# An attention and expert block on one core: the query scratch laid out anew, and the start in another order

## What is computed

```
mod = (silu(c) @ wmod)            # per sequence: shift, scale, gate, twice
h = layernorm(x) * (1 + ca) + sa
qkv = (h @ Wqkv.T + bqkv).reshape(B, 16, S, 24)      # a plain reshape
attn = softmax(q @ k.T / sqrt(8)); x = x + ga * ((attn @ v) @ Wo.T + bo)
h = layernorm(x) * (1 + cb) + sb
probs = softmax(h @ router_w.T); top 2 of 8 experts
x = x + gb * sum(w_i * (h @ expert_i + p_i))
```

## Time and profile before

| | |
|---|---|
| median of 3 runs | 556.86 us (556.68 to 558.76) |
| profiled execution | 557.98 us, of which the span in the profile is 556.1 us |
| ACT busy | 494.8 us, 89% |
| PE busy | 519.1 us, 93% |
| first exponential of tile 0 starts | 23.83 us |
| one tile in the loop | 15.7 us |
| packets | 85497, of which under 512 B 61508 |

### The profile page before, as it was taken

One profiled execution on the slowest core, in us unless ns is written; L12 is line 12 of the kernel. 1 busy time (PEld: TensorE's weight loads), 2 busy tenths in 40 slices (PEclk: granted clock), 3 DMA queues, 4 the chain that ended last, 5 costly groups with the idle time before them and its releaser, 6 DMA issues. The chain is left out here.

```text
span 556.1 us, 14357 instructions
## 1 busy us (share of the span) xinstructions
PE 519.1 (93%) x4064; PEld 215.3 (39%) x4064; DVE 362.8 (65%) x1271; ACT 494.8 (89%) x571; POOL 219.2 (39%) x429
## 2 busy tenths in 40 slices
PE   7488889999999999999999999999999999999983
PEld 6233333334343434343433333343434343433352
DVE  4435457677867666677767667677676666664466
ACT  1279989999999999999999999999999999998962
POOL 1223233344443334444443343444433344443335
PEclk9999999999999999999999999999999999999997
DMA  4573333333333333333333333333333332333010
GB/s 100 128 199 90 89 96 78 77 97 88 89 90 89 96 98 84 76 78 93 88 90 90 98 93 83 72 88 91 88 89 95 98 86 65 91 96 84 17 32 14
DMA packets 85497, 48.44 MB, mean 87 GB/s; under 512 B 61508, under 2 KB 76240, under 8 KB 85456
## 3 DMA queue, kind: packets, MB, share of 16 engines
q1 hardware_dynamic: 70162, 43.07, 30.0%
q10 hardware_dynamic: 15294, 4.82, 3.8%
HBM read 32.91 MB, written 14.94 MB: 86 GB/s over the span
## 5 line engine op out<-in xcount | busy, mean ns | idle before, releaser
L547 ACT ACTIVATE probs<-ps_scores 128x1024 f32<-128x1024 f32 x512 | 485.8, 1028 | 42.9 <-DMA q_scr<-qk_parts 19.6
L735 PE MATMUL ps_attn<-probs,values 128*32 128x512 f32 x2048 | 248.1, 599 | 0.4 <-issue 0.4
L717 PE MATMUL ps_scores<-query_stack,key_stack 32*128 32x512 f32 x1024 | 130.7, 500 | 17.5 <-ACT probs L547 11.4
L717 PEld LDWEIGHTS ps_scores<-query_stack,key_stack 32*128 32x128 f32 x1024 | 49.4, 183 | 167.9 <-ACT probs L547 164.1
L422 POOL TENSOR_SCALAR var_eps<-moments 128x1 f32<-128x1 f32 x64 | 12.3, 192 | 222.7 <-DVE moments L1078 149.5
L735 PEld LDWEIGHTS ps_attn<-probs,values 128*32 128x32 f32 x2048 | 54.0, 109 | 110.5 <-issue 110.3
L765 PE MATMUL ps_side<-experts_gated,h2T 128*128 (+1 forms) x228 | 74.7, 409 | 0.0
L1067 DVE RECIPROCAL sums_inv<-sums 128x128 f32<-128x128 f32 x32 | 30.5, 952 | 32.5 <-DMA attnT<-a_scr 32.5
L1074 DVE TENSOR_TENSOR x<-ps_side,x_gated 128x128 f32<-128x128 f32 x31 | 9.0, 292 | 60.8 <-PE ps_side L765 57.2
L1150 DVE TENSOR_TENSOR weighted<-ps_side,coef 128x256 f32<-128x256 f32 x114 | 46.5, 408 | 2.4 <-PE ps_side L765 2.4
L471 POOL TENSOR_TENSOR mix<-weighted 128x512 f32<-128x512 f32 x31 | 39.7, 1280 | 0.0
(11 more groups left out here) (129 smaller groups left out, 498.9 us busy)
## 6 DMA issues: line engine op xcount, KB each, us to landing
key_stack<-k_scr SPq DMA_DIRECT2D x128, 128.0 KB, 2.7
query_stack<-q_scr SPq DMA_DIRECT2D x121, 64.0 KB, 2.2
q_scr<-qk_parts SPq DMA_DIRECT2D x188, 32.0 KB, 2.0
k_scr<-qk_parts SPq DMA_DIRECT2D x64, 64.0 KB, 1.7
a_scr<-attn ACTq DMA_DIRECT2D x126, 18.0 KB
sums<-a_scr SPq DMA_DIRECT2D x32, 64.0 KB, 2.1
attnT<-a_scr SPq DMA_DIRECT2D x32, 64.0 KB, 2.2
out_dram<-out_all ACTq DMA_DIRECT2D x29, 64.0 KB, 1.8
```

Of the source, the lines that this page charges most:

```text
L547: nc.scalar.activation(probs[:, k % RING, g, :], ps_scores[:, slot(k, g), :], ACT.Exp, scale=SCALE)\
L717: mm = nc.tensor.matmul(out_, key_stack[p0:p0 + 32, parity, 2 * k:2 * k + 2, :].rearrange("p j r -> p (j r)"), query_stack[p0:p0 + 32, par ...
L735: mm = nc.tensor.matmul(ps_attn[q:q + 32, :], values[:, parity, g, k, :], probs[:, k % RING, g, h * HALF:(h + 1) * HALF], start=(k == 0), ...
```

## The change

**Scratch.** `q_scr` was `[2, G, 3, 64, R]`: for each half of the partitions and each head three slabs, high, low and high again. Six writes filled it, and a read took 16 rows and each of them together with the row 8 further on. It is now `[G, 2, hd, 2, JH, R]`: the high and the low row of a channel lie side by side. Four writes fill it, each from all 128 partitions. A read takes 16 rows in a row, and takes the whole set twice: its first index is now the repeat (2, step 0), then 16 rows. Before, the first index was 16 rows and the second the pair.

**Transfers.** Of the first tile's four writes ACT issues three and SP one (before four and two). The second tile's query reads go from ACT to the end of SP's prologue, ahead of the load of the remaining x.

**Order of the start.** DVE no longer waits for the value projection before it takes the first q and k from PSUM, since that projection writes to another bank. POOL's `squares` of tile 1 waits until `qk_parts` is done. `hT` of tile 2 is made ahead of the moments of tile 3 and the gate columns. The transposition for tile 3 and the norms of tile 2 move from the end of PE's prologue to behind the first scores of tile 0. `keep_warm` has five new calls, and one with a larger count.

```diff
-    q_scr = nc.dram_tensor("q_scr", [2, G, 3, P // 2, R], F32, kind="Internal").ap()
+    q_scr = nc.dram_tensor("q_scr", [G, 2, hd, 2, JH, R], F32, kind="Internal").ap()
...
-        def write_q(eng, n1, copies=range(6)):
+        def write_q(eng, n1, copies=range(4)):
...
-            for h in range(2):
-                rows = qk_parts[h * R:(h + 1) * R, 0].bitcast(F32).rearrange("p a (g r) -> p a g r", g=G)
-                for place, a in enumerate((0, 1, 0)):
-                    if 3 * h + place not in copies:
-                        continue
-                    eng.dma_start(q_scr[h, :, place].rearrange("g p r -> p g r"), rows[:, a]).then_inc(q_written, 16)
+            rows = qk_parts[:, 0].bitcast(F32)
+            for copy in copies:
+                g, a = copy // 2, copy % 2
+                halves = q_scr[g].rearrange("h d a i r -> a (h d) i r")[a]
+                eng.dma_start(halves, rows[:, a, g * R:(g + 1) * R]).then_inc(q_written, 16)
...
-                    parts = q_scr[h, g].rearrange("s (d i) r -> (s d) (i r)", d=hd)
-                    rows = bass.AP(tensor=parts.tensor, offset=parts.offset, ap=[[HALF, 2 * hd], [hd * HALF, 2], [1, HALF]])
+                    parts = q_scr[g, h].rearrange("d a i r -> (d a) (i r)")
+                    rows = bass.AP(tensor=parts.tensor, offset=parts.offset, ap=[[0, 2], [HALF, 2 * hd], [1, HALF]])
...
-                write_q(sp, 1, (4, 5))
+                write_q(sp, 1, (3,))
...
                 write_q(sp, 2)
                 read_k(2, 1)
+                read_q(sp, 2, 1)
...
             rstd(1, moments1, var_eps1, rstd1, "moments1_done", "var1_done", "rstd1_done")
+            reached(pool, ev["qk_parts_done"], 1)
             squares_of_tile(1)
...
-                    if k == 3 and before == 0:
-                        read_q(act, 2, 1)
...
-            write_q(act, 1, (0, 1, 2, 3))
+            write_q(act, 1, (0, 1, 2))
...
-                keep_warm(2)
+                keep_warm(3)
                 pe.wait_ge(w_loaded, 16)
...
+                if before == 0:
+                    reached(pe, ev["qkT_done"], 2)
+                    a_transpose(3)
+                    a_norms(ps_side[:, P + NE:P + NE + 2 * J], 2)
...
             a_transpose(1)
+            keep_warm(2)
             pe.wait_ge(setup_dve, SETUP_WQKV)
             a_project_qk(1, 0)
-            a_project_v(1, 0, 2 * P)
+            a_project_v(ps_scores[:, 2, HALF:HALF + P], 1, 0)
             setup_columns()
+            keep_warm(2)
...
             a_norms(ps_scores[:, 1, 0:2 * J], 1)
+            keep_warm(1)
             a_normT(ps_scores[:, 1, HALF:HALF + P], 1)
+            keep_warm(4)
             a_transpose(2)
             a_project_qk(2, 1)
-            reached(pe, ev["qkT_done"], 2)
-            a_transpose(3)
-            a_norms(ps_side[:, P + NE:P + NE + 2 * J], 2)
+            keep_warm(4)
...
                 a_hT(0, 1, 0)
                 dve.wait_ge(bias_cols_loaded, 16 * 3)
-                reached(dve, ev["v_ps_done"], 1)
                 a_qk(1)
...
                 a_bounded(ps_scores[0:1, 1, HALF:HALF + P], 1, 0)
+                a_hT(1, 2, 1)
                 a_moments(2, 3)
                 setup_columns()
-                a_hT(1, 2, 1)
```

More of the change, by code:

```diff
@@ L285, in write_q @@
             reached(eng, q_loaded, loaded_before)
-            for h in range(2):
-                rows = qk_parts[h * R:(h + 1) * R, 0].bitcast(F32).rearrange("p a (g r) -> p a g r", g=G)
-                for place, a in enumerate((0, 1, 0)):
-                    if 3 * h + place not in copies:
-                        continue
-                    eng.dma_start(q_scr[h, :, place].rearrange("g p r -> p g r"), rows[:, a]).then_inc(q_written, 16)
+            rows = qk_parts[:, 0].bitcast(F32)
[3 more added lines that the diff above has]
+                eng.dma_start(halves, rows[:, a, g * R:(g + 1) * R]).then_inc(q_written, 16)
         def read_q(eng, n1, parity, stacks=range(4)):
-            q_count, scores_before = times(eng, n1, 96), times(eng, plus(eng, n1, -2), 1)
+            q_count, scores_before = times(eng, n1, 64), times(eng, plus(eng, n1, -2), 1)
             reached(eng, scores_ready[KT - 1][G - 1], scores_before)
@@ L656, in a_project_qk, with a_project_v @@
                 mm.then_inc(ev["qk_ps_done"], 1)
-            def a_project_v(u1, ring, col):
+            def a_project_v(ps, u1, ring):
                 for n in range(G):
                     for odd in range(2):
-                        mm = nc.tensor.matmul(ps_side[odd * R:(odd + 1) * R, col + n * R:col + (n + 1) * R],
+                        mm = nc.tensor.matmul(ps[odd * R:(odd + 1) * R, n * R:(n + 1) * R],
                                               hT[:, ring, n * R:(n + 1) * R], wvT[:, odd].rearrange("p k d -> p (k d)"),
@@ L803, in side1 @@
                 if before >= 2 and after >= 1:
-                    a_project_v(at[2], 1 - parity, P)
+                    a_project_v(ps_side[:, P:2 * P], at[2], 1 - parity)
                 if past < 4 <= before:
@@ L821, in side2 @@
                 if before < 2:
-                    a_project_v(at[2], 1 - parity, 2 * P)
+                    a_project_v(ps_side[:, 2 * P:3 * P], at[2], 1 - parity)
                 if past < 3 <= before:
@@ L1003, in a_qk_parts @@
             def a_qk_parts(n, n1):
-                k_count, q_count = times(dve, n, 32), times(dve, n, 96)
+                k_count, q_count = times(dve, n, 32), times(dve, n, 64)
                 reached(dve, ev["qkT_done"], n1)
@@ L1011, in a_qk_parts, with a_values @@
                 v.tensor_tensor(qk_parts[:, :, 1], qkT[:], qk_parts[:, :, 0].bitcast(F32), ALU.subtract).then_inc(ev["qk_parts_done"], 1)
-            def a_values(u1, ring, col):
+            def a_values(ps, u1, ring):
                 reached(dve, ev["v_ps_done"], u1)
                 v.scalar_tensor_tensor(out=values[:, ring, :, :, 0:hd],
-                                       in0=ps_side[:, col:col + P].rearrange("p (g k d) -> p g k d", g=G, d=hd),
+                                       in0=ps.rearrange("p (g k d) -> p g k d", g=G, d=hd),
                                        scalar=VALUE_SCALE, in1=spread(bv[:], 1, G), op0=ALU.mult, op1=ALU.add)\
@@ L1228, in tile @@
                 if before >= 2 and after >= 1:
-                    a_values(at[2], 1 - parity, P)
+                    a_values(ps_side[:, P:2 * P], at[2], 1 - parity)
                 if past < 3 <= before:
@@ L1239, in tile @@
                 if before < 2:
-                    a_values(at[2], 1 - parity, 2 * P)
+                    a_values(ps_side[:, 2 * P:3 * P], at[2], 1 - parity)
                 if past < 3 <= before:
@@ L1325, in prologue @@
                 value_bias()
-                a_values(1, 0, 2 * P)
+                a_values(ps_scores[:, 2, HALF:HALF + P], 1, 0)
                 head_sums()
```

## The result

The changed kernel takes 586.62 us (median of 6 runs, 585.39 to 589.43), the kernel before 556.77 us (6 runs, 556.59 to 559.08): a ratio of 1.053 (95%: 1.050 to 1.056), 5.3% slower. I had forecast 556.9 us, no change. The profiled execution of the changed kernel took 589.43 us, its span is 587.6.

A forecast was written before the change was run, and what follows sets the result against it. A tile takes what ACT's 16 exponentials take, with PE close behind. Terms: + 1.9 (start) + 0.5 (norms) - 2.0 (reads off ACT) - 0.3 (second tile's reads) = + 0.1 us, forecast 556.9 us, 8-in-10 range 551.5 to 562.

The forecast's parts named there:

- the loop: Term for the loop's tiles: four query reads make attention rows 0 to 1.0 us late, nothing on the path.
- the two engines: Query reads with first index 2 run on two DMA engines of 16; four reads take 7.0 us, not 0.9.
- the slack: In a loop tile, DVE's result for PE may come 1.0 us late at no cost.
- the slower rival: Loop tiles pay for attention rows over 1.0 us late: 560 to 575 us, chance 0.20.
- the loop pays: The slower rival's title: beyond 1.0 us late, each 0.3 us per tile costs 8 us; chance 0.20.
- Reads at the start: First tile's query reads on two engines: first scores at 24.9, 1.9 us later than before.
- First parts: Start, first q and k parts: done at 10.95, 0.5 us gained (0 to 1.4), projection delayed about 0.5 us.
- The case of an early upper level: Start: if added matmuls bring the upper clock level before 8 us, 1.2 us gained.
- Inside tile 0: First tile: 0.5 us lost to moved transposition and norms, 2.0 gained at the ninth exponential by taking reads off ACT.
- The 0.5 us for the norms: Tile 0: transposition and norms behind the first scores cost 0.5 us, bounds 0 and 1.0.
- What would show it: Profile signs: query reads land after 4 to 9 us, scores near 25, unchanged 15.7 us tile, about 8200 packets fewer.
- that mark: Sign in the profile: a query read lands 4 to 9 us after issue; under 3 us would refute the forecast.

The follow-up runs named there:

- 12: 8 with ACT's four attention writes each two exponentials later: 577.47 us, ratio 1.037.
- Experiment 11: 8 with ACT's four attention writes each one exponential later: 555.12 us, ratio 0.997.
- 5: Changed kernel with head 0's query reads split into two transfers of 16 rows each, head 1's left on two engines: 561.84 us, ratio 1.009.
- 8: experiment 3 without the five added keep_warm calls, and one count of 3 back to 2: 555.57 us, ratio 0.9965.
- experiment 3: Changed kernel with each query read issued as two of 16 rows (32 KB each), new scratch and four writes kept: 555.28 us, ratio 0.997.
- experiment 1: Changed kernel with the old scratch, its six writes and 16-row-first reads; new start and second query read on SP kept: 556.10 us, ratio 0.9985.
- experiment 10: experiment 1 with the second tile's query reads back on ACT, behind its 8th exponential: 553.38 us, ratio 0.995.

## Why the prediction was wrong, point by point

*The step that failed* is the loop: "I expect 0 to 1.0 us late, nothing on the path." The mechanism, the two engines, was weighed right and the slack nearly right. The lateness was mis-sized, and with it the term of the sum, which I put at 0: the write lands 1.4 us late where 0.8 were free, and lateness of that size costs some 22 us over all tiles (12). The length of the reading was about right (forecast 8.4 us from the first read's issue to the end, measured 243.4 - 235.84 = 7.6). What I had wrong is what it delays. Against the slower rival I wrote that the last attention write is issued "when most of the reading is over". But its shares on the two engines come through only behind all of the query rows, and SP waits until the whole write has landed. By my own figures the reads ended at 243.3, already 1.1 us past the attention read at 242.18. Here a wait for a transfer was a wait for the slowest of its engines.

*The slack.* Where PE waits, in the changed kernel and in 12, side 0 runs 2.6 us after `sums_inv` starts (249.77 - 247.19); before, 3.36. So 0.8 us were free, where I had 1.0. Experiment 11 fits: with rows 0.5 us late PE still came without a wait (2.83 us), at 555.12. So does 5, with 0.47.

*The price.* The rival "the loop pays" had 0.3 us a tile in its sum and 560 to 575 as its bounds. Lateness alone cost 21.9 us (12 against 8), 0.7 to 0.8 us for each of the loop's and outer tiles; it was 1.6 us there, a little more than in the changed kernel. On top the changed kernel has the 3.0 us of the first reads and the 6.1 us of second gaps in the three spells: 31.0 us, and it is 31.3 slower than experiment 3. That a late side ends in a spell at the lower clock was in none of my cases. Why just these three tiles fell, and none in 12, stays open (PE's longest wait for `weighted` is 2.4 us in the changed kernel and 1.2 in 12).

*Reads at the start.* Forecast 1.9 us later, measured 2.0 (25.87 against 23.83), first scores at 25.04 against 24.9. That it came out so close is partly luck. Without the two engines I had the first scores at 20.5, and experiments 1, 3 and 8 have them at 22.15, 22.30 and 22.18. So the new start gains less than I thought, and the two engines cost some 3 us, not 4.4. The rule of the Trainium skill, "DMA: Bandwidth & Descriptors", section "Why a DMA increments its semaphore by 16 and not by 1", is that a transfer runs on the largest number of engines up to 16 that divides the slowest dimension of both of its sides. For the new reads that is two, and the trace agrees: 14.0% of 16 engines, 2.2, at 41 GB/s.

*First parts.* Forecast done at 10.95, measured 10.61: the two `keep_warm` matmuls moved the projection by 0.09 us (8.10 against 8.01), not 0.5, and DVE's subtraction took 0.43 us in place of 0.72. The case of an early upper level with 1.2 us gained exists: experiment 10's profile shows it.

*Inside tile 0.* The two terms, 2.0 us gained for taking the reads off ACT and 0.5 lost for the norms, left 1.5. From the first exponential to the ninth it took 10.98 us before and 10.20 in experiment 1, so 0.8 were gained. The gap in front of the ninth shrank from 2.48 to 1.17 us and did not go: PE's scores for it start 9.65 us after the first exponential in 1 and 8.70 before, so PE holds it now. I had let the ninth follow the old scores. The 0.5 us for the norms was right for its place: 0.6 between 8 and 9. In the changed kernel the gap in front of the ninth is 1.74 us.

*What would show it.* No landing time is given for the new reads in the DMA view, so that mark was no mark; the 15.7 us tile and the starts of the scores were. The tile changed by 0.6 us, and by my own words that says that the forecast is wrong. The packets fell by 85497 - 74489 = 11008, not by 8200; why stays open.

## What to carry to other kernels

Before an access pattern gets a small first index, find every other transfer whose landing somebody waits for while it runs: they share the engines, and here each landed with its slowest share. Put the same rows in two transfers instead, which here cost one queue more issues and nothing in time. And a slack is tested best by moving the late thing alone (experiments 11 and 12), and the lateness is then read from the trace and not from the edit: 0.5 us was free, 1.6 us cost 22 us.

## What the hardware showed that I had not expected

Four reads of 64 KB on two engines run at 41 GB/s, and an 18 KB write beside them took 1.4 us longer to land: the writes' last 54 packets came behind the last query rows. A PE that waited 1.3 to 2.4 us for a late input fell to a granted clock of 0.50 for 3.3 to 6.7 us in three tiles of the loop, and a PE that was busy 8.33 of 9.00 us at the start, in part with idle matmuls, was granted 0.50 from 12 to 21 us in one profiled execution.
